# A row-wise sum and reciprocal on VectorE, moved behind the masked product in a chunked gated-attention kernel

## The reference

```python
xn = _layernorm(x)
q = _swish(xn @ Wq); k = _swish(xn @ Wk); v = xn @ Wv
f = log_sigmoid(xn @ Wf) / 8.0; s = 1.0 - exp(f)
def step(carry, inp):                     # one token
    ge = jnp.exp(g_t)
    hk = hk * ge[:, :, None, :] + k_t[..., :, None] * s_t[..., None, :]
    logits = jnp.einsum('bhk,bhkm->bhm', q_t * scale, hk)
    p = jax.nn.softmax(logits, axis=-1)
    hv = hv * ge[..., :, None] + s_t[..., :, None] * v_t[..., None, :]
    o_t = jnp.einsum('bhm,bhmv->bhv', p, hv)
o = o * rsqrt(mean(o * o) + NORM_EPS) * g_norm_w
x = x + o @ Wo + sigmoid(xr @ W_r) * (square(relu(xk @ W_k)) @ W_v)   # xr, xk: xn mixed with the token before
```

## Time and profile before

| | us |
|---|---|
| two runs | 1880.4 and 2005.0 |
| median of the runs | 1942.7 |
| profiled execution | 1880.8 |
| its span, slowest core | 1879.2 |
| PE busy | 1275.9 (68%) |
| DVE busy | 789.4 (42%) |
| ACT busy | 511.5 (27%) |

### The profile page before, as it was taken

One profiled execution on the slowest core, in us unless ns is written; L12 is line 12 of the kernel. 1 busy time (PEld: TensorE's weight loads), 2 busy tenths in 40 slices (PEclk: granted clock), 3 DMA queues, 4 the chain that ended last, 5 costly groups with the idle time before them and its releaser, 6 DMA issues.

```text
span 1879.2 us, 22911 instructions; the slowest of 8 cores (1873.8 to 1879.2 us)
## 1 busy us (share of the span) xinstructions
PE 1275.9 (68%) x8093; PEld 779.3 (41%) x8172; DVE 789.4 (42%) x1825; ACT 511.5 (27%) x1105; POOL 81.7 (4%) x112
## 2 busy tenths in 40 slices
PE   1406595866859586785958677595867759586774
PEld 1303263544426353442625344362534436253442
DVE  2325435354343535434353543434354343435433
ACT  1102232322223232322323232232323223232322
POOL 1000000000000000000000000000000000000000
PEclk9857696877959687785968778595877859587785
DMA  5770000000000000000000000000000000000000
GB/s 169 241 267 23 12 12 34 12 23 23 23 12 12 34 12 23 23 23 12 12 34 12 23 23 23 12 12 34 13 23 23 23 12 12 34 13 23 23 1 23
DMA packets 19136, 65.77 MB, mean 35 GB/s; under 512 B 2256, under 2 KB 3664, under 8 KB 19024
## 3 DMA queue, kind: packets, MB, share of 16 engines
q0 software_dynamic: 12736, 47.19, 7.0%
q1 hardware_dynamic: 6288, 17.12, 2.5%
HBM read 47.52 MB, written 16.78 MB: 34 GB/s over the span
## 4 chain that ended last, share of the span: by engine, by line
PE 54%; DVE 20%; ACT 10%; issue 8%; DMA 5%; DVEq 1%; SPq 0%; ACTq 0%; POOL 0%; POOLq 0%
PE pB L167 18%; PE pA L167 15%; PE pC L167 8%; PE pF L167 5%; PE pD L167 3%; DVE hv L829 3%; PE pT L172 3%; PE pE L167 3%; DVE lnscr L296 2%; ACT xn_bf L887 2%; DVE fstage L583 1%; DVE tmp L578 1%; DVE hv_bf L834 1%; ACT L500 1%; ACT L389 1%
## 5 line engine op out<-in xcount | busy, mean ns | idle before, releaser
L167 PE MATMUL pC<-wo_sb,xn_bf 128*128 128x512 bf16 x225 | 103.0, 619 | 37.9 <-ACT xn_bf L887 33.3
L661 ACT ACTIVATE t_l<-t_e,t_linv 128x256 f32<-128x256 f32 x32 | 16.2, 508 | 364.1 <-DVE t_linv L644 364.1
L167 PE MATMUL pA<-wrt_sb,fstage 128*128 128x512 bf16 x240 | 58.5, 386 | 67.8 <-DVE xtail L468 67.0
L172 PE MATMUL pT<-identb_sb,xn_bf 128*128 128x128 bf16 x256 | 32.4, 307 | 90.5 <-DVE xnT L359 48.6
L492 DVE TENSOR_TENSOR Am_sb<-pD,mask_sb 128x512 bf16<-128x512 f32 x16 | 11.1, 692 | 179.3 <-PE pD L167 179.2
L167 PE MATMUL pD<-v_sb,spp 128*64 128x256 bf16 x64 | 19.6, 409 | 97.0 <-ACT o_bf L801 97.0
L172 PE MATMUL pT<-identb_sb,k_sb 128*128 128x128 bf16 x256 | 32.6, 268 | 75.4 <-ACT kT_sb L675 75.4
L507 DVE CAST l_hi<-t_l 128x512 bf16<-128x512 f32 x16 | 6.8, 427 | 182.0 <-ACT t_l L503 182.0
L906 DVE TENSOR_TENSOR ob<-pC,fstage 128x512 f32<-128x512 f32 x32 | 22.1, 692 | 137.9 <-PE pC L167 137.9
L167 PE MATMUL pF<-wo_sb,xn_bf 128*128 128x512 bf16 x256 | 79.9, 467 | 0.0
L887 ACT COPY xn_bf<-pT 128x512 bf16<-128x512 bf16 x64 | 34.5, 589 | 157.6 <-PE pT L172 157.4
(11 more groups left out here) (162 smaller groups left out, 2656.3 us busy)
## 6 DMA issues: line engine op xcount, KB each, us to landing
out<-ob POOLq DMA_DIRECT2D x32, 512.0 KB, 2.9
xb<-x POOLq DMA_DIRECT2D x30, 512.0 KB, 4.2
stage<-wq POOLq DMA_DIRECT2D x2, 1024.0 KB, 8.5
fstage<-wq SPq DMA_DIRECT2D x2, 1024.0 KB, 8.9
fstage<-wk SPq DMA_DIRECT2D x2, 1024.0 KB, 5.6
stage<-wk POOLq DMA_DIRECT2D x2, 1024.0 KB, 6.6
fstage<-wv SPq DMA_DIRECT2D x2, 1024.0 KB, 6.9
stage<-wv POOLq DMA_DIRECT2D x2, 1024.0 KB, 6.5
```

The lines of the kernel that those rows point to most:

```text
L167: e.matmul(out=o, lhsT=l, rhs=r, start=st, stop=sp),
L172: lambda e, o=out_ap, i=in_ap, d=ident: e.transpose(out=o, in_=i, identity=d),
L661: em("scalar", lambda e: e.activation(out=sm_e, in_=sm_lg, func=AF.Exp, scale=SCALE, bias=nmS4[:, 0:1]), waits=[("V", nms_done)], inc="S")
```

## The change

The two DVE instructions that make ssm4 and rs4 are emitted later: not between Pt_sb and the copy of its transpose, but after the masked product Bm_sb, as the last two of `emit_R_ha`. Their operands and their form stay as they are. Nothing else is edited, so `bm_done=val("V")` in the return, which stood right behind Bm_sb, now stands behind the reciprocal.

```diff
@@ -681,11 +681,6 @@
                 out=Pt_sb[:], in0=sm_e, in1=lam_sb[:, j * 256:(j + 1) * 256], op=ALU.mult),
                waits=[("S", sme_done), ("V", val("V"))], inc="V")
             pt_done = val("V")
-            em("vector", lambda e: e.reduce_sum(
-                out=ssm4, in_=sm_e.rearrange("p (h m) -> p h m", h=4), axis=AX),
-               waits=[("V", val("V"))])
-            em("vector", lambda e: e.reciprocal(out=rs4, in_=ssm4), waits=[("V", val("V"))],
-               inc="V")
 
             bank = ptb(0)
             for h in range(4):
@@ -710,6 +705,11 @@
                                                    in1=mask4[:], op=ALU.mult),
                waits=[("T", b_done)], inc="V")
             reader(pB, "V")
+            em("vector", lambda e: e.reduce_sum(
+                out=ssm4, in_=sm_e.rearrange("p (h m) -> p h m", h=4), axis=AX),
+               waits=[("V", val("V"))])
+            em("vector", lambda e: e.reciprocal(out=rs4, in_=ssm4), waits=[("V", val("V"))],
+               inc="V")
             return dict(c=c, first=first, par=par, j=j, bm_done=val("V"),
                         pt_done=pt_done, kt_done=kt_done,
                         rs4=rs4, v2_=v2_, v3_=v3_, sc4=sc4)
```

## The result

| | us |
|---|---|
| before, median of 8 runs | 1883.3 |
| after, median of 9 runs | 1897.6 |
| ratio after to before | 1.0084, 95% interval 1.0072 to 1.0097 |
| profiled execution after, slowest core | 1896.8, span 1895.2 |
| mean granted clock of the slowest core, before and after | 0.763 and 0.765 |

The change costs 0.84%, which is 15.8 us of the 1880.8 that the forecast started from. The forecast was 25.7 us. In some executions the cores of a die are slower by some per cent at a lower granted clock, whatever the kernel; the ratio leaves these out, and is therefore not quite that of the two medians.

The account below looks back on a forecast made before the run. The prediction took a chain handing over between PE (54%) and DVE (20%), neither full, as the bound. It added 32 x 0.804 = 25.7 us to 1880.8, with 0 for removal and clock: 1906.5 us, range 1896 to 1923.

Parts of the forecast that it names:

- What the removal gives: Behind Pt_sb the pair is hidden under PE's transposes, so taking it away gains 0.2 us at most, taken as 0.
- What the pair costs: Behind Bm_sb, sum 0.420, reciprocal 0.178 and two hand-overs of 0.103 make 0.804 us for one chunk.
- Chunk 0: bm_done and DVE's queue: In chunk 0, bm_done names the reciprocal and later DVE work queues behind it; pD starts 0.80 us late, 16 times.
- Chunk 1: the row of DVE work ahead of hv_bf: In chunk 1 the pair delays L808, the hv updates and so pD's wait for hv_bf: 0.80 us, 16 times.
- The sum: Over the whole kernel, 32 x 0.804 = 25.7 us on 1880.8, giving 1906.5 us.
- What is uncertain: the clock: TensorE's clock changes within superchunks; bounds -0.22 to +0.96 us in each of 15, -3 to +14 us, taken as 0.
- rival D: Not slower: later starts meet earlier clock rises, giving back 1.6 us per superchunk; end at 1881 to 1885; chance 0.09.
- A: The forecast: both places exposed, clock neutral; 1906.5 us, own range 1900 to 1914; chance 0.66.
- B: Only one of the two places is exposed, most likely chunk 0; 1893.7 us; chance 0.08.
- The range: Whole-kernel time from 1896 to 1923 us, holding A with what the clock may do to it, and C.
- C: The clock makes it worse, most superchunks meeting a later rise; 1920.9 us, 1923 or beyond if missed; chance 0.14.
- What the profile would show: Chunk 0's pD about 0.95 us behind Bm_sb, chunk 1's hv_bf waits 3.6 us, superchunks of 110.6 to 111.2 us.

Follow-up runs that it names:

- e4: The kernel after with both instructions, row sum and reciprocal, deleted; ratio 1.0002 to before.
- d2: The kernel before with two extra small reciprocals behind Bm_sb and ahead of bm_done in every chunk; ratio 1.0031.
- w6: The kernel before, pair behind Pt_sb, with matmuls nobody reads put on PE where it waits; ratio 0.9181, 1728.5 us.
- f1: Against before: pair at the head of emit_R_hb, and the lbc matmul, lbc_sb and spp moved ahead of the pD and pE matmuls; ratio 0.9738.
- d6: The kernel before with six extra small reciprocals behind Bm_sb and ahead of bm_done in every chunk; ratio 1.0295.
- w2: The changed kernel with the same unread matmuls in PE's waits as w1; ratio 0.9545 to before.
- w1: The kernel with the pair at the head of emit_R_hb, plus matmuls nobody reads in PE's waits; ratio 0.9262 to before.

## Why the prediction was wrong in size, step by step

- **What the removal gives: 0.** Right. After, the copy waits 25.7 us longer for PE, and without the pair (e4) the time stays.
- **What the pair costs, 0.804 us.** Right to 0.01: 15.21 to 16.01 and 15.27 to 16.07 in the windows. The sentence that the prediction takes from the Trainium skill (VectorE: DVE Perf Modes, section on the DRAIN you can't avoid) compares eight copies with a semaphore behind each and with one behind the last only, and finds the same time for both. It does not say that there is no gap between two instructions, so it is no rule against the 0.103 us that the trace has ahead of each of the pair.
- **Chunk 0: bm_done and DVE's queue.** Right; pD 0.95 us behind Bm_sb, released by the reciprocal. **Chunk 1: the row of DVE work ahead of hv_bf.** Right; 0.82 us on each of 16 waits.
- **The sum, +25.7 us.** Wrong by 10 us. The failed step is "What is uncertain: the clock", where I took 0 and bounded it at -0.22 us per superchunk. It measured -0.51 (1.10 instead of 1.61 us), and -0.90 with less added (d2: 0.22 instead of 1.12).
- **Why that bound was bad.** I took the spread of the lengths for what the clock can do. But the spread was small because the clock evens lengths out, not because it has no hold on them. In w6, core 4, with the granted clock at 1.00, the twelfth and thirteenth whole superchunks take 99.40 and 99.05 us, 0.71 and 0.36 more than the eleventh; in before, core 0, they take 109.47 and 109.11 (the pair in the earlier trace rows), only 0.33 more than the eleventh and 0.03 less. The rows had a hint that I put under rival D and gave 0.09: 109.47 followed by 109.11. I rejected D with "the best superchunk seen gave back 0.22 us", which is the same mistake. D's mechanism is what happened, in part, and a part was what no rival priced: A's own range began at 1900 and D's ended at 1885. B's 1893.7 came closest by number, for a reason that the windows rule out, since both places pay. D's price should have been read from the projections: in before, core 0, they took 4.7 to 6.3 and 5.0 to 6.3 us for the same matmuls, so more than 1 us was there to be had in each.
- **The range.** Its lower end was 1896, and the median is 1897.6. That it lies inside is luck: with the bound of -3 us that I gave the clock, the sum could not come below 1903, and no term stands behind the rest of the way down to 1896. C was right in kind, too: second projections that miss their rise take 1.1 us more, and this is part of why after does not stay at 109.3. But its superchunks had to be 111.8 us (110.19 and the pair) as a rule, and the longest of the 112 is 111.41.
- **What the profile would show.** Of "superchunks of 110.6 to 111.2 us" only a part is there; four of core 6's 14 are at 109.3 to 109.4.

The mechanism fits a sentence of the Trainium skill (TensorE: Matmul & The Clock Gate, section on what is actually happening, in part 1): the monitor behind the clock runs freely, so the place of a rise in the work depends on where the work lands. The runs agree, and add what a loop makes of it: projections that start later in the superchunk meet their rise sooner (3.2 us in, not 5.1), get shorter, and so the superchunk falls back into step. The same section puts the ramp of the clock at under 1% of a typical kernel's span. It says so of the matmuls at a kernel's start, and it is no price for a loop in which the clock falls and rises in every pass: here the clock decided 10 of 26 us, and holding it high was worth 8%.

## What to carry to other kernels

A wait that is taken from a counter (`val("V")` in a return) moves with whatever is emitted before it: look for it when instructions are moved, and keep it next to the instruction that it is for. A chain of waits that runs through two engines that end together names one of them by hundredths of a microsecond; take the later of the other candidates before counting a gain. Where a loop's PE clock rises and falls inside each pass, do not add or subtract small costs straight: measure the PE-bound stretch just behind the clock's rise, and compare stretch by stretch, since the total can hide a cost that the next change will bring out.

## What the runs showed of the hardware that I had not expected

- Eight independent cores, each with its own start, settle at the same superchunk lengths, most of them 109.1 to 109.5 us, and keep them with 0 to 1.1 us of work added. With less or more work they settle at about 105.9 (f1) or 112.6 (d6).
- Idle PE time costs twice: 95 unread matmuls per superchunk (w6), put into waits, raised the mean granted clock from 0.76 to 0.97 and made the kernel 8.2% faster (w6) without shortening any chain of work. The output projections went from 5 to 6 us each to 3.8 and 3.5.
- With eight cores at work in dense projections the granted clock read 0.99 or 1.00 over that stretch of 51.4 us, in before as in w6. In the first 250 us of some executions it read a third level on two or four of the cores: in w6, core 4, it was 0.81 from 160 to 220 us. In the superchunks whose windows are shown it does not occur.
- With the pair behind Bm_sb in both chunks the clock fell in 111 of the 112 superchunks of w2, where w1 kept it in 79. In 83 of them it fell ahead of the wait that the pair adds in chunk 0, so the cause is not simply that wait.
